# K transposed: built from symmetric similarities and a transposed adjacency, in place of TensorE transposes of K

## The reference

```python
z_l, z_g, v = h @ W_lang.T, h @ W_grav.T, h @ W_V.T        # h = x[b], 512 x 512, for each of 16 batches b
zn  = z_l / max(norm(z_l), EPS)
A_l = max(zn @ zn.T, 0) * not_eye
d2  = max(sq + sq.T - 2 z_g @ z_g.T, 0)                     # sq = row sums of z_g squared
A_g = exp(-d2 / (2 sigma^2)) * not_eye
K_l, K_g = rows of (A_l * adj), (A_g * adj), each row divided by its sum
K   = w_l K_l + (1 - w_l) K_g
x   = layernorm(x + K @ v @ W_O.T)
```

## Time and profile before

| | us |
|---|---|
| median of 3 runs | 1019.85 (1018.96 to 1020.45) |
| profiled execution: span from the first to the last instruction | 1016.6 |
| what lies around that span, against the median | 3.25 |
| PE busy | 1002.1 (99%) |
| DVE, ACT, POOL busy | 646.2 (64%), 322.4 (32%), 151.8 (15%) |

### The profile page before, as it was taken

The page is one execution under the profiler, slowest core; times in us unless marked ns, Lnnn a source line. Parts: engine busy times, 40 slices in busy tenths (PEclk is TensorE's granted clock), DMA queues, the critical chain, the costliest instruction groups (busy, mean ns, idle before and its releaser), DMA issues.

```text
span 1016.6 us, 15123 instructions
## 1 busy us (share of the span) xinstructions
PE 1002.1 (99%) x5194; PEld 867.0 (85%) x5194; DVE 646.2 (64%) x1786; ACT 322.4 (32%) x632; POOL 151.8 (15%) x155
## 2 busy tenths in 40 slices
PE   9999999999999999999999999999999999999997
PEld 7788888888888888888888889888898888888885
DVE  4565757657485674757757586574856748477488
ACT  4333233232422333233232332324233232242341
POOL 1202111021200212102021100212001121010231
PEclk9999999999999999999999999999999999999999
DMA  8320130403104040140401304031040401403001
GB/s 218 72 43 1 46 80 5 121 0 94 31 21 104 0 117 7 42 84 0 124 0 59 66 11 113 0 97 28 21 103 0 114 11 42 83 0 125 1 21 63
DMA packets 155378, 55.04 MB, mean 54 GB/s; under 512 B 133824, under 2 KB 137920, under 8 KB 155328
## 3 DMA queue, kind: packets, MB, share of 16 engines
q1 hardware_dynamic: 153216, 53.49, 20.9%
q10 hardware_dynamic: 2112, 1.05, 0.4%
HBM read 37.75 MB, written 16.78 MB: 54 GB/s over the span
## 4 chain that ended last, share of the span: by engine, by line
issue 66%; PE 20%; POOL 11%; DVE 2%; POOLq 0%; DMA 0%; ACT 0%; DVEq 0%
POOL mask_r L1014 6%; PE ring L283 5%; PE ring L285 5%; PE ring L284 4%; POOL rstd L1021 3%; PE g_bank L283 2%; PE g_bank L285 2%; PE g_bank L284 2%; POOL r L1008 1%; PE g_bank L278 1%; PE ring L278 1%; POOL u_odd_lo L996 1%; PE g_bank L321 0%; DMA y<-in_x_dram 0%; DVE al L823 0%
## 5 line engine op out<-in xcount | busy, mean ns | idle before, releaser
L660 DVE TENSOR_TENSOR zl_lo<-ring,zl_hi 128x512 fp32r<-128x512 f32 x64 | 44.1, 691 | 117.3 <-ACT zl_hi L525 117.3
L569 ACT ACTIVATE off<-g_bank 128x128 f32<-128x128 f32 (+1 forms) x128 | 40.4, 331 | 227.8 <-DVE diag_out L736 227.3
L1021 POOL TENSOR_TENSOR rstd<-var_eps,neg_half 128x1 f32<-128x1 f32 x64 | 46.0, 719 | 410.2 <-DVE var_eps L855 410.2
L283 PE MATMUL ring<-xT_hi,wgT_hi 128*128 128x512 f32 x256 | 101.6, 397 | 0.0
L283 PE MATMUL ring<-xT_hi,wlT_hi 128*128 128x512 f32 x256 | 101.4, 396 | 0.0
L283 PE MATMUL ring<-wvo_hi,xT_hi 128*128 128x512 f32 x256 | 101.0, 395 | 0.0
L285 PE MATMUL ring<-xT_hi,wlT_lo 128*128 128x512 f32 x256 | 99.9, 390 | 0.0
L285 PE MATMUL ring<-wvo_hi,xT_lo 128*128 128x512 f32 x256 | 99.8, 390 | 0.0
L285 PE MATMUL ring<-xT_hi,wgT_lo 128*128 128x512 f32 x256 | 99.8, 390 | 0.0
L284 PE MATMUL ring<-xT_lo,wgT_hi 128*128 128x512 f32 x256 | 99.8, 390 | 0.0
L284 PE MATMUL ring<-xT_lo,wlT_hi 128*128 128x512 f32 x256 | 99.8, 390 | 0.0
(11 more groups left out here) (121 smaller groups left out, 2248.8 us busy)
## 6 DMA issues: line engine op xcount, KB each, us to landing
xb<-in_x_dram SPq DMA_DIRECT2D x60, 256.0 KB, 4.7
out_dram<-y SPq DMA_DIRECT2D x60, 256.0 KB, 2.0
y<-in_x_dram SPq DMA_DIRECT2D x14, 1024.0 KB, 5.7
y<-in_x_dram SPq DMA_DIRECT2D x4, 256.0 KB, 5.3
al<-in_L_gnn_W_grav_dram ACTq DMA_DIRECT2D x4, 256.0 KB, 5.9
ag<-in_L_gnn_W_lang_dram SPq DMA_DIRECT2D x1, 1024.0 KB, 9.8
xb<-in_L_gnn_W_V_dram SPq DMA_DIRECT2D x1, 1024.0 KB, 11.9
mask_r<-in_L_gnn_W_O_dram SPq DMA_DIRECT2D x4, 256.0 KB, 9.1
```

The costliest lines, as they stand in the source:

```text
L283: nc.tensor.matmul(psum, lh, rh, start=k == 0, stop=False)
L569: nc.scalar.activation(off[:, mine[0]:mine[-1] + 1, :], g_bank[i][:, j0 * P:(j0 + len(mine)) * P] .rearrange("p (c n) -> p c n", n=P), ACT ...
L660: nc.vector.tensor_tensor(pair[1][:, i, :], bank[:, :], pair[0][:, i, :].bitcast(F32), ALU.subtract).then_inc(evacuated, 1)
L1021: nc.gpsimd.tensor_tensor(rstd[:, i:i + 1], var_eps[:, i:i + 1], neg_half[:, 0:1], ALU.pow)\
```

## The change: what it does

K is no longer turned on TensorE. Since the two similarity matrices are symmetric, K transposed is the similarity times the transposed adjacency times a scale for each column. So the kernel loads the adjacency a second time in blocks at the start, transposes it on DVE (`maskT`, four instructions) and clears its diagonal on POOL. In each batch:

- `sum_ag` and `sum_al` still use `mask`, but only for row sums (their product goes to `mask_s`, which nobody reads). `al` is now copied out of PSUM by ACT with a Relu (`copy_al`); ACT also clamps the exponents' arguments (`clamp`).
- Two more columns, `scale_g` and `scale_l`, are widened by ACT, turned by one TensorE matmul each ("pg" and "q", `scale_as_rows`) and laid along `scale_row` by DVE (`repeat_row`).
- POOL multiplies `ag` by `maskT` (`turn_ag`) and by `scale_row` (`scale_kg`), and `maskT` by the second `scale_row` (`scale_maskT`).
- DVE's `combine` is two instructions for each row tile; ACT's `hi_k` and DVE's `lo_k` split K transposed in SBUF.
- On TensorE `transpose_k` is gone. A tile of K transposed holds one k step of all four `out` tiles, so `aggregate_pair` does `out` 0 and 1 together, k step by k step, as the tiles come; `out` 2 and 3 follow.

The core of the diff:

```diff
-BATCH = ([("zg", 1, 0), ("hsq", 0, 0), ("zg", 1, 1), ("zg", 1, 2), ("zg", 1, 3), ("zl", 1, 0), ("r", 0, 0),
-          ("zl", 1, 1), ("zl", 1, 2), ("zl", 1, 3), ("u", 1, 0), ("u", 1, 1), ("u", 1, 2), ("kT", 0, 0),
-          ("u", 1, 3), ("kT", 0, 1), ("out", 0, 0), ("kT", 0, 2), ("out", 0, 1), ("kT", 0, 3), ("out", 0, 2),
-          ("out", 0, 3)])
+BATCH = ([("zg", 1, 0), ("hsq", 0, 0), ("zg", 1, 1), ("zg", 1, 2), ("zg", 1, 3), ("pg", 0, 0), ("zl", 1, 0),
+          ("r", 0, 0), ("zl", 1, 1), ("zl", 1, 2), ("zl", 1, 3), ("u", 1, 0), ("q", 0, 0), ("u", 1, 1), ("u", 1, 2),
+          ("u", 1, 3), ("out", 0, 0), ("out", 0, 1), ("out", 0, 2), ("out", 0, 3)])
...
+LAST = (BATCH[:11]
+        + [("q", 0, 0), ("u", 1, 0), ("hsq", 1, 0), ("u", 1, 1), ("u", 1, 2), ("out", 0, 0), ("r", 1, 0), ("pg", 1, 0),
+           ("out", 0, 1), ("out", 0, 2), ("out", 0, 3), ("q", 1, 0), ("u", 1, 3), ("out", 1, 0), ("out", 1, 1),
+           ("out", 1, 2), ("out", 1, 3)])
...
-                def transpose_k(self, db, i):
-
-                    bank = self.begin(("kT", db, i))
-                    pe.wait_ge(k_ready, (self.b + db) * T + (i + 1))
-                    transposed(bank, [al[:, i, j * P:(j + 1) * P] for j in range(T)]).then_inc(stream_ready, 1)
+                def aggregate_pair(self, db, parity):
+
+                    for i in range(2):
+                        self.begin(("out", db, i))
+                    for k in range(T):
+                        pe.wait_ge(kT_split, (self.b + db) * T + (k + 1))
+                        for i in range(2):
+                            self.out_step(db, i, k, parity)
...
+                s.project("u", 0)
+                s.scale_as_rows("q", 0)
+                for i in range(1, T):
                     s.project("u", i)
...
+                s.aggregate_pair(0, parity)
+                s.aggregate(0, 2, parity)
+                s.aggregate(0, 3, parity)
...
+                    nc.vector.scalar_tensor_tensor(
+                        out=mask_s[:, i, :], in0=self.al(db)[:, i, :], scalar=1.0, in1=mask_s[:, i, :],
+                        op0=ALU.mult, op1=ALU.mult, accum_out=sum_l[:, i:i + 1]).then_inc(al_summed, 1)
...
                 def combine(self, db, i):
 
-                    dve.wait_ge(ag_scaled, self.rows(db, i))
+                    dve.wait_ge(mask_q_ready, self.rows(db, i))
+                    al_i = self.al(db)[:, i, :]
+                    nc.vector.tensor_tensor(al_i, al_i, mask_s[:, i, :], ALU.mult).then_inc(al_scaled, 1)
+                    dve.wait_ge(al_scaled, self.rows(db, i))
+                    dve.wait_ge(kg_ready, self.rows(db, i))
                     nc.vector.scalar_tensor_tensor(
-                        out=al[:, i, :], in0=al[:, i, :], scalar=scale_l[:, i:i + 1], in1=ag[:, i, :],
+                        out=al_i, in0=al_i, scalar=r[:, i:i + 1], in1=ag[:, i, :],
                         op0=ALU.mult, op1=ALU.add).then_inc(k_ready, 1)
...
+                s.sum_al(0, 0)
+                s.sum_al(0, 1)
+                s.sum_al(0, 2)
                 s.lo("zl", 1, 2, zl)
...
+                s.sum_al(0, 3)
+                s.scale_of_al(0)
                 s.lo("zl", 1, 3, zl)
...
+            def until_q(b, stream):
+                turn_ag(b)
+                inverse_norms(b)
+                scale_kg(b, stream, 0, range(2))
+                scale_mask(stream, 0)
+                scale_kg(b, stream, 0, range(2, T))
+                scale_maskT(b, stream, 0)
```

More of the change, by code:

```diff
@@ L467, in last_two @@
             def last_two(b, stream):
                 s = Steps(b, stream)
[L469 to L479, removed]
-                s.project("u", 0)
-                pe.wait_ge(evacuated, stream.upto(("zg", 1, T - 1)))
@@ L600, in until_zl @@
                 s.hi("zg", 1, 0, zg)
+                s.clamp(0, 0)
+                s.clamp(0, 1)
                 s.exp(0, 0)
@@ L714, in _ @@
                     x_transpose(1, k + 2)
-            dve.wait_ge(scalar_step, 5)
+            dve.wait_ge(adj_blocks_loaded, 16 * QN)
+            for k in range(T):
+                nc.vector.transpose(maskT[:, k, :], adj_turned[:, k, :]).then_inc(maskT_transposed, 1)
+            dve.wait_ge(scalar_step, 6)
             dve.wait_ge(ident_ready, 1)
@@ L800, in mask_al, with sum_al @@
+                def sum_al(self, db, i):
+                    if db and i < 2:
+                        dve.wait_ge(last_mask_r_ready, i + 1)
+                    else:
+                        dve.wait_ge(mask_r_ready, (self.b + db) * T + (i + 1 - 2 * db))
+                    dve.wait_ge(al_copied, self.rows(db, i))
                     nc.vector.scalar_tensor_tensor(
[L801 to L802 removed]
@@ L920, in last_two @@
                 until_zl(s)
+                s.diagonals(1, gg_rows, 0.5, hsq, gg_diag)
+                s.repeat_row("q", 0)
+                s.combine(0, 0)
                 s.lo("u", 1, 0, u[1])
-                for i in range(T):
-                    s.combine(0, i)
-                s.diagonals(1, gg_rows, 0.5, hsq, gg_diag, range(T - 1))
-                s.lo("kT", 0, 0, kT)
-                s.diagonals(1, gg_rows, 0.5, hsq, gg_diag, [T - 1])
-                s.lo("kT", 0, 1, kT)
-                s.residual(0, 0)
@@ L938, in last_two @@
-                s.mask_ag(1, 0)
-                s.residual(0, 1)
-                s.row_sums(0, 1)
-                s.mask_ag(1, 1)
-                s.normalise(0, 0)
-                s.statistics(0, 1)
-                s.mask_ag(1, 2)
+                s.lo_k(0, 2)
+                s.lo("u", 1, 2, u[1])
+                s.lo_k(0, 3)
+                for i in range(T):
+                    s.sum_ag(1, i)
+                s.scale_of_ag(1)
                 s.diagonals(1, gl_rows, 1.0, nsq, gl_diag)
@@ L961, in last_two @@
-                s.mask_al(1, 3)
-                s.scale_of_al(1, first=1, earlier=1)
+                s.residual(0, 0)
+                s.repeat_row("r", 1)
+                s.scale_mask(1, 0)
+                s.scale_mask(1, 1)
+                s.repeat_row("pg", 1)
+                for i in range(T):
+                    s.sum_al(1, i)
+                s.scale_of_al(1)
+                s.residual(0, 1)
+                s.row_sums(0, 0)
+                s.statistics(0, 0)
+                s.residual(0, 2)
@@ L969, in last_two @@
-                s.lo("kT", 1, 1, kT)
-                s.row_sums(0, 3)
-                s.statistics(0, 2)
-                s.statistics(0, 3)
+                s.lo_k(1, 2)
+                s.lo_k(1, 3)
+                for i in (2, 3):
+                    s.row_sums(0, i)
+                    s.statistics(0, i)
                 s.normalise(0, 2)
@@ L1013, in scale_mask, with turn_ag, scale_kg, scale_maskT @@
                 for i in range(first, T):
-                    nc.gpsimd.tensor_tensor(mask_r[:, i, :], mask[:, i, :], row[:, :], ALU.mult)\
+                    nc.gpsimd.tensor_tensor(mask_s[:, i, :], mask[:, i, :], row[:, :], ALU.mult)\
                         .then_inc(mask_r_ready, 1)
+            def turn_ag(b):
+                for i in range(T):
+                    pool.wait_ge(ag_summed, b * T + (i + 1))
+                    nc.gpsimd.tensor_tensor(ag[:, i, :], ag[:, i, :], maskT[:, i, :], ALU.mult).then_inc(ag_turned, 1)
+            def scale_kg(b, stream, db, row_tiles):
+                pool.wait_ge(evacuated, stream.upto(("pg", db, 0)))
+                for i in row_tiles:
+                    pool.wait_ge(ag_turned, (b + db) * T + (i + 1))
+                    nc.gpsimd.tensor_tensor(ag[:, i, :], ag[:, i, :], scale_row[:, :], ALU.mult).then_inc(kg_ready, 1)
+            def scale_maskT(b, stream, db):
+                pool.wait_ge(evacuated, stream.upto(("q", db, 0)))
+                for i in range(T):
+                    pool.wait_ge(al_summed, (b + db) * T + (i + 1))
+                    nc.gpsimd.tensor_tensor(mask_s[:, i, :], maskT[:, i, :], scale_row[:, :], ALU.mult)\
+                        .then_inc(mask_q_ready, 1)
             def inverse_deviations(b, row_tiles=range(T)):
```

352 lines of the change are left out of this document (195 added, 157 removed).

## The result

The changed kernel takes **1128.73 us** (median of four runs; 1127.07 is the lowest) against 1019.75 for the kernel before on the same chip: 1.107 times as long, with a 95% interval of 1.105 to 1.108. Forecast were 1114.8 and a range of 1045 to 1140.

A forecast was written before the change was run, and what follows sets the result against it. TensorE, busy 99% of the span, was taken as the bound. Span 1016.6 + 71 (loop batches) + 24 (last two batches) = 1111.6, plus 3.25 around the span: 1114.8 us, range 1045 to 1140.

The forecast's parts named there:

- the chain: Loop batches, through "q" to K's tiles: each batch 5.07 us longer, 71 us for the loop's 14.
- the edge: The loop's six jumps back: no cost foreseen, 0 us in the sum.
- TensorE saves 1.38 a batch: Four K tiles no longer turned save 1.72 us, two added columns cost 0.34; 22.1 us in all if TensorE never waits.
- DVE and POOL take turns: DVE instructions with both inputs in SBUF alternate with POOL's tiles: 1.26 us a POOL tile, 0.61 a DVE instruction.
- Waits of 6.45 a batch: TensorE waits 2.05 us at "q", then 2.3, 1.35 and 0.75 for K's tiles in the `out` pair.
- From there in turns: From `sum_al` 0 at 521.24, DVE's sums alternate with POOL's mask and `scale_kg` tiles until 528.75; "q" can start at 530.0.
- About half a microsecond before `mirror_g` would wait: cost 0, and 1 a batch if that cover goes: DVE's work after `out` ends some 3.5 us later against TensorE, yet stays hidden ahead of the next mirrored blocks.
- Last two, 24: Last two batches: 29 us of TensorE waits, less 2.8 saved and about 2 of present waits; bounds 10 to 32.
- The clock falls: Rival: waits of 2 us a batch drop TensorE's clock to half, 86 us more, 1200 us; chance 0.05.
- Half of it: Rival: "q" comes in time, only K's tiles are late; 3.0 us a batch, 20 at the end, 1082; chance 0.14.
- No turns, but DVE's order: Rival: only waits of 0.25 and 0.55 us at K's tiles, about 10 lost in the last two, 1022; chance 0.07.
- The signs named beforehand: Profile after: PE busy about 91%, waits about 2 us at "q" and 4 on `out`, slower SBUF products, DVE under 75%.

The follow-up runs named there:

- the last experiment: the run with POOL's product ahead of "q", plus DVE steps reordered in the loop and last two batches and one wait for three `out` banks: 1009.16 us, 0.989 times before.
- the small products: Changed kernel with POOL's sixteen products of a batch cut to 8 of 512 columns, so K is not scaled: 1059.72 us, 1.040 times the kernel before.
- the sums from PSUM: Changed kernel with `sum_al` reading the z_l gram rows from PSUM instead of the copy in SBUF: 1109.86 us, 1.089 times the kernel before.
- the run with sums from PSUM and the loop written out: Changed kernel with `sum_al` reading PSUM and the batch-pair loop unrolled without jumps: 1071.27 us, 1.051 times the kernel before.
- the run with POOL's product ahead of "q": The run with sums from PSUM and the loop written out, plus POOL multiplying `al` by `maskT` before "q" and three `out` tiles together: 1022.53 us.

## Why the prediction was right, and where not

**Direction: right. Size: near, by luck.** One term of the sum is too large and one is missing: the chain was put at 71 and is 47.6, the edge at 0 and is 37.8. The two errors, -23 and +38, have opposite signs, so the total came out within 14 us of 1128.7. Of the 3.25 added for what lies around the span, 1.9 are there in the profiled run (1128.34 less 1126.4).

**TensorE saves 1.38 a batch: right, nearly.** It is 1.29 in the last experiment. To cost a transpose by the distance of starts, not by its 272 ns, was the choice that mattered: the durations would have promised 62 us in all, nearly 4 a batch.

**DVE and POOL take turns: right,** shown by the small products (1.41 to 0.685 us for `sum_al`) and by the sums from PSUM (the same fall with POOL's tiles at full size). The Trainium skill (SBUF — State Buffer, "Who interferes with whom") says that a DVE instruction with two SBUF inputs and a GpSimd one that reads SBUF block each other, and that the order of issue decides who waits. The trace agrees, and adds that when both have work queued they alternate, one instruction each.

**Waits of 6.45 a batch: over-sized,** 4.57 measured. The step that failed is "From there in turns": it let every instruction of DVE meet a full POOL tile, while the first of each group slipped in between two tiles. The bound given for it, 1 us a batch, was too narrow.

**"About half a microsecond before `mirror_g` would wait: cost 0, and 1 a batch if that cover goes": wrong,** and the largest error. That DVE would end 3.5 us later against PE was right. What was missed is that the cover was already used up at every second batch: the trace of before has the mirrored blocks waiting 0.7 and DVE pausing for 1.60 without a releaser just behind the jump, and the prediction uses neither row. The wait grew by 3.6, the clock fell in it, and 6.3 us a jump followed. The Trainium skill (Runtime: NRT & Kernel Launch, "Instruction fetch mechanics") has the rule: a taken branch to a place outside the stretch of instructions at hand breaks the fetch ahead, and execution stalls until they are fetched. DVE's trace agrees, with 2.94 and 2.01 us and the instruction queue's packets beside them; the jumps of POOL, ACT and SP, some 0.2 us each, show no such stall.

**Last two, 24: right in the number alone,** 23.2. The waits were over-sized (29, measured 19.8), and 7.2 us that were not in the sum, the lower clock among them, made up for it. That, too, is luck.

**The rivals.** "The clock falls" was a half truth. It did not fall at waits of 1.7 us, with the clock at 1.00 in 548 to 604. It fell behind each of the six of 4.3 to 4.5, at 2.1 for each beside the 0.7 at the blocks, and at 2.2, in the runs with sums from PSUM, in some batches. "Half of it", q in time and only the tiles late, is the run with sums from PSUM and the loop written out: it saves 0.9 a batch, not 2.05, since the wait at "q" was 1.4 and the tiles then wait longer. "No turns, but DVE's order" named 0.25 and 0.55 at the second and third tile; with POOL almost idle they measure 0.75 and 0.49.

**The signs named beforehand** came as said but for four: the wait at "q" is 1.2 to 1.4, not 2; those on `out` are 3.2 a batch, not 4; DVE is at 75%, the bound given, not under it; and a granted clock below 0.95 in the middle of the run, named as a sign of being wrong, is there behind each jump (0.50 in 610.4 to 614).

## What to carry to other kernels

Look at each boundary of a loop apart: the batch that ends at the jump has less cover than the one in the middle, and a mean or a single batch hides it. Before work is sent from TensorE to DVE and POOL, list which of their instructions read SBUF on both sides and lie on the chain between two matmuls; the same products placed ahead of the chain's last link cost little here (1022.5 against 1071, with `out` taken by threes as well). And if a saving is covered by a chain of other engines, the gain appears only when the last wait of that chain is gone: a batch became 3.40 longer, then 0.18 shorter, and at last 1.29 shorter, near the 1.38 of the sum.

## What had not been expected of the hardware

Small DVE instructions with a single SBUF tensor as input are held up by POOL too, but not all. From the run with POOL's product ahead of "q":

```profile
520.37 1.21 DVE L846 TENSOR_SCALAR deg<-deg 128x4 f32<-128x4 f32 x1
521.62 0.18 DVE L848 RECIPROCAL deg<-deg 128x4 f32<-128x4 f32 x1
...
521.52 2.54 POOL L1089 TENSOR_TENSOR al<-al,maskT 128x512 f32<-128x512 f32 x2
```

The 128x4 maximum (TENSOR_SCALAR, L846) has one tensor and a constant; it takes 1.21 and ends at 521.58, where POOL passes to its next tile, and 0.17 in the run with small products (means of 16: 1.214 and 0.170). The reciprocal, also with one input, takes its usual 0.18 in the middle of a tile. The forecast's rule of two SBUF inputs was too narrow. The section of the SBUF page of the Trainium skill named above has `tensor_scalar` among the instructions that can take both ports, on conditions; this trace agrees.

That a jump costs DVE about 5 us, 0.82 of which show in the time of the kernel before, was not expected either; writing the loop out made that kernel 0.5% faster with no other edit. Why the second packet of instructions comes as late as it does, and whether the 1 MB load that runs beside it (188 GB/s in 604 to 610.4) delays it, was not tried.
